# Perceiver stack on one core: turned rows ahead of a key and value unit, 25 units ahead of the second cross-attention, last latent pair by token halves

## The reference

```
x = x + cross_attention_0(LN(x), ctx)      # 16 heads, int8-like rounding
x = x + diff_attention(LN(x))              # 16 heads, difference of two softmaxes
x = x + gated_ffn(LN(x))                   # fp8 gate and up, gelu, fp8 down, hidden 1024
x = x + cross_attention_1(LN(x), ctx, mask)# 16 heads of 16, normalised result
x = x + latent_attention(LN(x))            # low-rank queries and keys, rotary part, causal
x = x + squared_relu_ffn(x)                # fp8-like scaling
```

## Time and profile before

| | us |
|---|---|
| median of 3 runs | 664.64 (663.59 to 665.05) |
| profiled execution | 665.43 |
| its span, first to last instruction | 663.6 |
| TensorE busy | 637.4 (96%) |
| VectorE busy | 421.4 (63%) |
| ScalarE busy | 274.5 (41%) |
| GpSimd busy | 59.0 (9%) |

### The profile page before, as it was taken

How to read it: one execution, slowest core, us unless ns; L and a number is a source line. 1 busy time by engine, 2 the same in 40 slices (tenths; PEclk the granted TensorE clock), 3 DMA queues, 4 the chain that set the end, 5 groups by cost and what they waited for, 6 DMA issues and landing times.

```text
span 663.6 us, 21569 instructions
## 1 busy us (share of the span) xinstructions
PE 637.4 (96%) x9568; PEld 427.7 (64%) x9570; DVE 421.4 (63%) x981; ACT 274.5 (41%) x502; POOL 59.0 (9%) x130
## 2 busy tenths in 40 slices
PE   9999999999988999999999999999999999999976
PEld 4666667567565566666666666777767775466754
DVE  2744468587765656555554773554888965787487
ACT  3454445445442233434333844544454454011134
POOL 1020000001001111011111003000010101000000
PEclk9999999999999999999999999999999999999999
DMA  7241111117005410001003612110182100000001
GB/s 241 65 171 63 35 34 55 44 35 224 2 3 202 149 34 26 16 27 33 2 2 89 210 52 64 34 67 34 60 260 97 67 4 1 3 3 2 3 1 33
DMA packets 28957, 42.25 MB, mean 64 GB/s; under 512 B 6080, under 2 KB 18880, under 8 KB 28352
## 3 DMA queue, kind: packets, MB, share of 16 engines
q1 hardware_dynamic: 28720, 40.60, 19.1%
q10 hardware_dynamic: 144, 0.26, 0.1%
HBM read 40.33 MB, written 0.52 MB: 62 GB/s over the span
## 4 chain that ended last, share of the span: by engine, by line
PE 83%; DVE 11%; issue 2%; ACT 2%; DMA 1%; POOL 0%; SPq 0%; DVEq 0%; ACTq 0%
PE psum L396 16%; PE psum L388 16%; PE psum L1146 7%; PE psum L476 6%; PE psum L441 5%; PE psum L451 4%; PE psum L1197 4%; PE psum L1152 4%; PE psum L1882 2%; PE psum L426 2%; PE psum L1861 2%; PE psum L1167 2%; PE psum L1842 1%; PE psum L1181 1%; DVE arena L1978 1%
## 5 line engine op out<-in xcount | busy, mean ns | idle before, releaser
L396 PE MATMUL psum<-arena 128*128 128x256 f32 x512 | 121.6, 384 | 0.1
L388 PE MATMUL psum<-arena 128*128 128x512 f32 x248 | 117.8, 602 | 0.0
L396 PEld LDWEIGHTS psum<-arena 128*128 128x128 f32 x512 | 93.9, 190 | 22.0 <-issue 9.0
L388 PEld LDWEIGHTS psum<-arena 128*128 128x128 f32 x248 | 43.4, 190 | 41.0 <-issue 39.2
L700 ACT ACTIVATE arena<-arena 128x512 f32<-128x512 f32 x64 | 47.8, 804 | 35.5 <-DVE arena L826 35.5
L694 ACT ACTIVATE arena<-psum,arena 128x512 f32<-128x512 f32 x64 | 40.2, 687 | 31.0 <-DVE arena L813 30.9
L1146 PE MATMUL psum<-y_cols,arena 128*128 128x512 f32 x112 | 52.9, 605 | 0.0
L476 PEld LDWEIGHTS psum<-arena 128*17 128x17 f32 x4096 | 38.5, 96 | 20.1 <-issue 13.0
L826 DVE TENSOR_SCALAR arena<-psum 128x512 f32<-128x512 f32 x64 | 39.7, 681 | 17.9 <-PE psum L441 17.9
L1249 ACT ACTIVATE arena<-psum 128x512 f32<-128x512 f32 x48 | 28.2, 597 | 48.2 <-PE psum L1146 30.9
L813 DVE TENSOR_REDUCE arena<-psum 128x1 f32<-128x512 f32 x64 | 39.7, 683 | 12.8 <-PE psum L426 12.5
(11 more groups left out here) (249 smaller groups left out, 932.7 us busy)
## 6 DMA issues: line engine op xcount, KB each, us to landing
arena<-in_ctxT SPq DMA_DIRECT2D x31, 512.0 KB, 3.7
arena<-in_L_attn_Wv SPq DMA_DIRECT2D x1, 2048.0 KB, 8.3
arena<-in_L_attn_Wq SPq DMA_DIRECT2D x8, 256.0 KB, 3.0
arena<-in_L_attn_Wk SPq DMA_DIRECT2D x8, 256.0 KB, 3.6
arena<-in_L_attn_Wo SPq DMA_DIRECT2D x1, 2048.0 KB, 12.3
arena<-in_L_ffn_w_gating SPq DMA_DIRECT2D x1, 2048.0 KB, 7.8
arena<-in_wo_rows SPq DMA_DIRECT2D x2, 1024.0 KB, 5.1
arena<-in_wq_upT SPq DMA_DIRECT2D x2, 768.0 KB, 7.7
```

Source lines behind the costliest of these rows:

```text
L388: last = nc.tensor.matmul(bank, wkv[:, c, i * P:(i + 1) * P], x[:, c, :], start=(c == 0), stop=(c == NC - 1))
L396: last = nc.tensor.matmul(bank[:, kk * D:(kk + 1) * D], x[:, c, k * P:(k + 1) * P], wkv[:, c, D:2 * D], start=(c == 0), stop=(c == NC - 1))
```

## The change

It has four parts. In F0, TensorE's turns and ScalarE's copies of the turned rows stand ahead of unit 6 instead of behind it. Unit 20 goes to the end of F0, and `FIRST` is 25: X1's opening does units 21 to 24, and batch 0 of the loop does units 25 and 26 (two in place of three); from batch 1 on every unit is where it was. At the end of X1, VectorE writes the last tile's normalised rows ahead of the head latents, and ScalarE copies pair 6's fold after the last tile's columns. In M1, the last pair's values are made for token tiles 0 and 1 and then, into banks 0 and 1 (`OB2`), for tiles 2 and 3; ScalarE copies the first half, VectorE the second (`last_oT`), and the output rows of the second half wait for that copy.

```diff
-    FIRST, FULL = 16 if L0 else 24, 10
+    FIRST, FULL = 16 if L0 else 25, 10
...
-            u = FIRST + 3 * min(b, FULL) + 2 * max(b - FULL, 0) + k
-            return None if k >= (3 if b < FULL else 2) or u >= 4 * NB else u
+            u = FIRST + 3 * min(b, FULL) + 2 * max(b - FULL, 0) - min(b, 1) + k
+            return None if k >= (3 if 0 < b < FULL else 2) or u >= 4 * NB else u
...
             next_cols(act, NT - 1)
+            guest(act, 4)
...
         next_stats(v, last)
+        next_rows(v, last)
         if not L0:
             guest(v, 2)
-        next_rows(v, last)
...
     def pe(pe):
+        for k in range(2):
+            norm_turn(nc, pe, e, f, k, TB[k])
         for u in units(6):
             e.phases[X1].unit_pe(pe, u)
-        for k in range(2):
-            norm_turn(nc, pe, e, f, k, TB[k])
...
-        for u in units(17, 18, 19):
+        for u in units(17, 18, 19, 20):
             e.phases[X1].unit_pe(pe, u)
 
     def act(act):
+        for k in range(2):
+            norm_cols(nc, act, e, f, k, TB[k], y8, saturate=False)
         for u in units(6):
             e.phases[X1].unit_act(act, u)
-        for k in range(2):
-            norm_cols(nc, act, e, f, k, TB[k], y8, saturate=False)
...
-        for u in units(15, 16, 17, 18, 19):
+        for u in units(15, 16, 17, 18, 19, 20):
             e.phases[X1].unit_act(act, u)
...
-    OB = e.psum[:, 2:4, 0:2 * P]
+    OB, OB2 = e.psum[:, 2:4, 0:2 * P], e.psum[:, 0:2, 0:2 * P]
...
-    def values(pe, j):
+    def values(pe, j, tiles=range(NT), OB=OB):
...
-        for t in range(NT):
+        for t in tiles:
...
         for k in banks:
+            if k and j == PAIRS - 1:
+                pe.wait_ge(s_pT, PAIRS + 1)
...
-        values(pe, PAIRS - 1)
+        values(pe, PAIRS - 1, (0, 1))
+        values(pe, PAIRS - 1, (2, 3), OB2)
         out_rows(pe, PAIRS - 1, 0, 1)
...
-            for j in range(2, PAIRS - 1):
+            for j in range(2, PAIRS - 2) if k == 3 else (PAIRS - 2,):
                 copy_fold(act, j)
...
+    def oT_part(j, bank, tiles=slice(0, NT)):
+        return (oT[j % 2].rearrange("p (t r x) -> p r t x", r=2, x=64)[:, :, tiles],
+                bank.rearrange("p r (t x) -> p r t x", x=64)[:, :, tiles])
+
     def copy_oT(act, j):
         act.wait_ge(s_pv, j + 1)
         wait(act, s_rows, 2 * (j - 1))
-        nc.scalar.activation(oT[j % 2].rearrange("p (t r x) -> p r t x", r=2, x=64),
-                             OB.rearrange("p r (t x) -> p r t x", x=64), ACT.Identity, scale=vvec).then_inc(s_oT, 1)
+        out, src = oT_part(j, OB, slice(0, NT // 2 if j == PAIRS - 1 else NT))
+        nc.scalar.activation(out, src, ACT.Identity, scale=vvec).then_inc(s_oT, 1)
+
+    def last_oT(v):
+        v.wait_ge(s_pv, PAIRS + 1)
+        v.wait_ge(s_rows, 2 * (PAIRS - 2))
+        out, src = oT_part(PAIRS - 1, OB2, slice(NT // 2, NT))
+        nc.vector.tensor_scalar(out, src, vvec, None, ALU.mult).then_inc(s_pT, 1)
...
         for j in range(PAIRS):
             softmax(v, j)
+        last_oT(v)
```

## The result

The changed kernel takes 661.89 us (median of 19 runs, 660.62 to 664.68) against 664.65 (19 runs, 663.59 to 667.52) for the kernel before: a ratio of 0.9958 with a 95% interval of 0.9947 to 0.9969, 2.8 us less (2.1 to 3.5). The forecast was 662.0, range 661.0 to 663.8. The profiled execution took 662.02, its span 660.2.

What follows compares the result with a forecast made beforehand. TensorE, busy for 96% of the span, was taken to bound the kernel except at the seams between phases. Terms of -0.93, -1.01, -0.17 and -0.55 sum to -2.66 us, taking 664.64 to 662.0, range 661.0 to 663.8.

Steps and rivals of the forecast that it cites:

- seam 1: Into the first feed-forward: turns before unit 6 let it cover ScalarE's copies, so gate products start sooner, -0.93 us.
- seam 2: Into the second cross-attention: unit 20 fills TensorE's idle time before the first turn, batch 0 is shorter, -1.01 us.
- hole: TensorE's lost time at the second cross-attention's first turn: 0.82 waiting plus 0.19 standing start, 1.01 us.
- seam 3: Into the latent attention: ScalarE copies the last token tile before pair 6's folds, -0.17 us; VectorE's earlier rows buy nothing.
- seam 4: Latent attention's end: pair 7's values by token halves start bank 0's output rows sooner, -0.55 us (0.45 to 0.66).
- spare at the clips: Batch 0, second cross-attention: VectorE's clips end 2.0 us before the second scores want them.
- latents' spare: End of the second cross-attention: head latents finish later on VectorE, still 1.3 us before TensorE wants them.
- my bounds: ScalarE's half copy of the last pair: between 0.37 and 0.58 us, halfway 0.48, against 0.70 now.
- A: Rival: batch 0 needed its third unit (-0.94, 663.7 us), or another term fails; together 20%.
- B: Rival: the edits do nothing, the fed gaps reappearing further on at VectorE; 664.6 us, 5%.
- C: Rival: new TensorE instruction-supply stalls; one of 1.5 us leaves -1.2, three give +1.8; 5% for anything slower than 664.6.

Runs made afterwards that it cites:

- single seams: Four kernels, each the kernel before with one seam's part of the diff alone: ratios 1.0001, 0.9997, 1.0003 and 0.9997.
- seam 1 alone: The kernel before with only the turns and their copies moved ahead of unit 6: ratio 1.0001, 664.49 us of 12 runs.
- seam 2 alone: The kernel before with only unit 20 moved to the first feed-forward's end, 25 units ahead, two in batch 0: ratio 0.9997, 664.01 us.

## Why the prediction was right

| term | predicted | measured in the profiles |
|---|---|---|
| seam 1, turns before unit 6 | -0.93 | -1.10 |
| seam 2, hole filled by unit 20 | -1.01 | -1.01 |
| seam 3, ScalarE's order | -0.17 | -0.20 |
| seam 4, halves | -0.55 | -0.45 |
| sum | -2.66 | -2.76 |

*What bounds it.* The stream through the second cross-attention had no slack, so what the first two seams gave arrived at its end: batches 1 to 15 keep their length but for the stop near 490 (119.29 before, 119.97 after, 0.66 of which is that stop). Right.

*Seam 1* was 0.17 too small. I set the new start on the chain's clock, 363.60, against 364.53, which is the row of a standing start. In a stream a row of the timeline begins about 0.16 before the one ahead of it has ended (units 4 and 5 end at 356.79 + 3.60 = 360.39, the turns begin at 360.23); after a wait it does not. So this removed wait gave back its idle time and the overlap: 0.94 + 0.16 = 1.10. At seam 2 I had counted it, as the 0.19 between the first turn and the second, and the sum came out exactly.

*Seam 2*: the condition was that nothing in batch 0 needed the third unit, with 2.0 spare at the clips; it was 1.95. With the spare cut by one further unit, 1.72, there was 0.23 left and still no wait.

*Seam 3*: the cause was ScalarE's order and VectorE's bought nothing, each shown alone. The wait fell by 0.21 where I had 0.17, because the copy followed the turn by 0.03 and not 0.05 and took 0.38 and not 0.40. The latents' spare was put at 1.3 and was 1.2.

*Seam 4* was 0.10 too large, and in the values, not in the copy. I took half of the 0.67. But the first 16 products take 0.44 to their end, as the chain of waits of the kernel after has it:

```profile
624.62 0.44 PE psum L1875 x16
625.08 0.48 ACT arena L1962
...
625.60 1.15 PE psum L1885 x4
```

That gives 0.23 and not 0.33. Put as a fixed part and a part for each product, 0.44 for 16 and 0.67 for 32 mean 0.21 fixed (an estimate from these two rows), and halving the products does not halve it; what it consists of no row shows. The copy took 0.48, the middle of my bounds, 0.70 - 0.48 = 0.22. The warning of the Trainium skill ("VectorE: DVE Perf Modes", "The TRN2 errata") is given for instructions that read SBUF. These copies read PSUM, so no run here tests it in its own case. A fixed part shows in their rows all the same, 0.47 + 0.48 busy against 0.70; but since only the first half is on the path, it decides nothing here, whichever engine does the second.

*Rivals.* A and B fell on the rows above. C, new stops of instruction supply, was right only in that the stops exist. Their lengths differ from execution to execution (none to 1.22 near 490), they were there before, and nothing measured ties them to the edits. Their cause, instruction loading or another, was not tried.

*Luck in the number.* Seams 1 and 3 gave 0.17 and 0.03 more than forecast and seam 4 gave 0.10 less, which partly cancel. The forecast of 662.0 rests on the median of three runs and lies 0.1 from the measured 661.89, while the measured gain is only known to 0.7 either way. So close a hit is in part chance, and so is it that the medians differ by the same 2.76 as the seams.

*Open.* The single seams' times do not add up to the whole: their ratios differ from 1 by +0.0001, -0.0003, +0.0003 and -0.0003, in sum -0.0002, where the whole is -0.0042. The four half-widths of 0.0012 to 0.0014 give 0.0025 in quadrature, and more, as all four share one set of runs before; the gap of 0.0040 lies at the edge of what chance makes likely, and seam 1's expectation is missed by its own interval. The profiles, one execution for each kernel, show each seam's gain in full.

Dips of the granted clock, told of in the last section, explain a part. In six of the twelve runs of seam 1 alone the mean granted clock was 0.997 or less, with a median of 665.7; of the 35 runs of before in the same comparison six were at 0.998 or less, median 666.6. Taking only runs at 0.999 or 1.000, the medians differ from before's 664.57 (29 runs) by -0.75 (seam 1, 6 runs), -0.66 (9), +0.37 (8) and +0.02 (10): in sum -1.0. Drawing the runs anew many times puts that sum between -2.8 and +0.6 (an estimate from the same runs, chosen after the fact). With all runs it is -2.5 to +2.3. Both take in no gain as well as nearly the whole of the seams' 2.76, so the times of single seams are too coarse to tell. The changed kernel's second set of runs, taken in the same way, is 2.0 under before's (662.35 of 9 runs against 664.34 of 13). That the edits work together in a way that no profile shows is not excluded.

## What to carry to other kernels

Where an engine is full but for a wait at each seam between phases, put work that depends on nothing new behind the step that starts the next engine and not ahead of it, and enough of it to fill the wait: here one unit ahead of the turns cost 1.1 us, filling the hole gave 1.0, and one unit more gave nothing. The unit was 0.71 longer than the hole, and that cost nothing only because the same unit was taken out behind it, where the other engines had time to spare. Ask of each reordering which engine's row ends last there; of the two in seam 3, only ScalarE's paid. And read an effect of a few tenths from the length of its seam in the profile, where two profiles of one kernel agreed within 0.02 us, since the whole run wanders by some 4 (663.35 to 667.73 in 35 runs of the kernel before).

## What the runs showed of the hardware

TensorE's granted clock fell for a few microseconds in some executions. Windows of 2 us in the profile of seam 2 alone, in code that none of the edits touch (busy us of TensorE, weight loads, VectorE, ScalarE, GpSimd; granted clock; DMA share; GB/s):

```profile
196.00:198.00 2.00, 1.08 (x19) 0.79 (x19) 0.00 (x0) 0.66 (x3) 0.00 (x0) 1.00 0.00 0
198.00:200.00 2.00, 2.00 (x7) 1.05 (x6) 1.57 (x5) 0.10 (x2) 0.00 (x0) 0.69 0.04 8
200.00:202.00 2.00, 2.00 (x5) 1.09 (x4) 1.22 (x5) 0.00 (x0) 0.00 (x0) 0.50 0.00 0
...
208.00:210.00 2.00, 1.44 (x9) 1.38 (x9) 0.00 (x0) 0.74 (x2) 0.00 (x0) 0.75 1.00 403
210.00:212.00 2.00, 2.00 (x10) 1.81 (x9) 0.00 (x0) 1.43 (x3) 0.00 (x0) 0.50 1.02 412
```

At 0.50 it is at the lower of its two levels, 1.2 GHz of 2.4. It fell after a stretch in which TensorE had been busy 1.08 of 2 us, and once more after one of 0.69 of 2 us at 206 to 208. The kernel before was busy 0.95 and 0.69 us in the same two windows and kept 1.00, so the same program text meets it in one execution and not in another. The profile with both halves on ScalarE has a dip in the same code, 0.50 at 200 to 202 and 0.73 at 202 to 204. What a dip costs: from the stop near 196 to unit 4, a stretch with the same instructions, the profile of seam 2 alone has 163.0 us (195.50 to 358.54) and the first of the kernel before 160.4 (196.95 to 357.39), 2.6 more.
